# Issuing one of two row transfers from ScalarE's instruction stream instead of SyncE's, in a transformer layer on one core

## The chip, the core and the metric

The kernel runs on one core of a Trainium2 chip. A core has five engines with an instruction stream each: TensorE (PE in the rows, with its weight loads as PEld), VectorE (DVE), ScalarE (ACT), GpSimd (POOL) and SyncE (SP), which computes nothing and issues transfers. Transfers run on 16 DMA engines that all streams share. The streams meet only at semaphores. The metric is the device time of one execution in microseconds (us); lower is better.

## What is computed

A post-norm transformer layer on x of shape (4, 1024, 128) in float32: causal attention with 16 heads of size 64, a residual, a layer norm, a feed-forward part whose hidden layer of 512 passes butterfly transforms, a second residual and layer norm. The change is in the attention alone:

```python
q = einsum('BSE,EHK->BSHK', x, w_q);  k, v likewise
logits = einsum('BSHK,BMHK->BSHM', q, k) / sqrt(64)
probs = softmax(logits + causal_mask, axis=3)
out = einsum('BSHK,BMHK->BSHK', probs, v)
x = layernorm(x + einsum('BSHK,EHK->BSE', out, w_o))
```

## The kernel before

Work goes in 32 **units**: a unit is one pair of heads of one batch entry (8 units for each of 4 entries). All streams are written out by hand, unit by unit, by a function `window` on each engine; a function `flush` on each stands at the end of a batch entry (output projection, residual, statistics), so between units 8, 16 and 24 and their predecessors lies that other work.

Within a unit there are 12 steps (`STEPS`): two chunks of 512 queries, and for each the key tiles of 128 that the mask leaves. In a step TensorE makes the scores of head 0 and then of head 1, each from two matmuls: line 662 (high part of the keys by high part of the queries, into the PSUM tile `SC`) and line 666 (`KH1` by `QL`, into the same tile). ScalarE takes the exponential of each (line 867, `PR<-SC`), GpSimd masks and sums (lines 500 to 523), TensorE multiplies with the values (line 683).

**Where the maxima come in.** The softmax subtracts each query's maximum. It is known before the unit starts: while TensorE works on unit u it also computes the raw scores of unit u+1 (line 634), VectorE reduces them (lines 989 and 992) into `NEGM`, TensorE transposes that (line 639, the filler `mt`), and VectorE copies it out of PSUM into `NROW` (line 1002), 16 partitions of 128 numbers: 8 for head 0, 8 for head 1. `QL` holds, for each head, 64 partitions with the low part of the queries and one more partition, a row of 1024 numbers, for the negated maxima; against it `KH1` has a row of ones. So the matmul of line 666 adds the negated maximum to the scores at no cost, but cannot start until the row is in `QL`. **A row of `QL` lies in one partition, `NROW` in eight, so a DMA has to carry it**: two transfers of 4 KB for each unit, one a head, both from `rows` (line 394) in SyncE's stream. Both count on the semaphore `m_landed`, and TensorE waits for both before the first line 666 of a unit (line 665). Nothing else of that unit's scores can go ahead of it.

**What lies around it.** A unit is long (about 31 us); its last three steps are short. The fillers that TensorE works off between the steps are listed by step in `FILL`: at step 9 the projection `("proj", 0, 0)` (queries of a later unit) and behind it `mt`; at step 11, behind both scores, `("proj", 2, 0)`: three matmuls on lines 614 to 616, whose result ScalarE copies to `VT` (line 807). After it comes the next unit with its lines 662 and 666. ScalarE's stream has the same order: exponentials of step 10, of step 11, the copy to `VT`, then the next unit's first exponential.

**SyncE's stream** for a unit: `copies` (lines 381 and 385, four pairs of 128 KB), `inverses` of the denominators (lines 402, 406 and 409), `rows` for the next unit, and in 18 of the units `stage_weights` (line 364, 512 KB into `SW`) behind them; then the next unit's `copies`.

Of the kernel before, what the change touches and what calls it, by code (L numbers as in the profile page):

```python
# [24 lines left out]
F32 = mybir.dt.float32  # L25
# [5 lines left out]
H, K = 16, 64  # L31
PAIRS = H // 2
UNITS = B * PAIRS
TILES = S // P
# [35 lines left out]
def adds_reading(s):  # L70

    return adds_until(s + 2 if STEPS[s][1] == 0 else s + 1)
# [90 lines left out]
def post_norm_layer(nc, x, w_q, w_k, w_v, w_o, W_exp, b_exp, up_w, up_b, down_w, W_con, b_con, down_b, out):  # L163
    ctx = ExitStack()
    with ctx:
        def sb(name, shape, dt=F32):
            return ctx.enter_context(nc.sbuf_tensor(name, shape, dt))

        def sem(name):
            return ctx.enter_context(nc.semaphore(name))  # L170
# [9 lines left out]
        QL = sb("QL", [P, 2, 2, S], F32R)  # L180
# [16 lines left out]
        NROW = sb("NROW", [2 * TILES, P], F32R)  # L197
# [61 lines left out]
        negm_made, nrow_made, m_landed = sem("negm_made"), sem("nrow_made"), sem("m_landed")  # L259
# [15 lines left out]
        def lays_after(n):  # L275

            return [CHUNKS + (n - 8) // 2] if n >= 8 and n % 2 == 0 and CHUNKS + (n - 8) // 2 < len(LAY) else []
# [9 lines left out]
        def unit_at(b, j, par):  # L287
            return At(par, PAIRS, 2, b, j)
# [4 lines left out]
        FIRST, MIDDLE, PENULTIMATE, LAST = range(4)  # L293
# [10 lines left out]
        def work_base(b, j, par, kind):  # L304

            return At(len(PREFETCH) + NF * par - (kind != FIRST) - (len(EARLY) if kind == LAST else 0)
                      - (LAYS if b == B - 1 else 0), PER_BATCH, 2 * NF, b, j)
# [7 lines left out]
        def fillers(kind):  # L315

            n, made = 0, []
            for s, place, f in FILLERS:
                if kind == FIRST and f == ("norm", 1, 1):
                    continue  # L320
                if (kind == PENULTIMATE and f in EARLY) or (kind == LAST and f[0] != "norm"):
                    continue
                made.append((s, place, f, n, 1 + (f in EARLY)))
                n += 1
            return made
# [5 lines left out]
        def pair_col(j, par, ahead):  # L331

            return ((j * 2 + (par + ahead)) % PAIRS) * P
# [6 lines left out]
        def prob(unit, s, n=None):  # L340

            qc, kt = STEPS[s]
            n = CH - START[s] if n is None else n
            return PR[:, (unit.times(NS) + s) % PRING, :, 0:n]
# [5 lines left out]
        def _(sp):  # L350
# [37 lines left out]
            def rows(par, f_unit):  # L388

                sp.wait_ge(nrow_made, (f_unit + 1).value())  # L390
                for h in range(2):
                    row = K if h == 0 else 0
                    dst = QL[row:row + 1, par, h, :].rearrange("a (t c) -> a t c", t=TILES)
                    sp.dma_start(dst.bitcast(F32), NROW[h * TILES:(h + 1) * TILES, :].bitcast(F32)).then_inc(m_landed, 16)  # L394

            def inverses(unit, qc):

# [405 lines left out]
        @block.scalar  # L804
        def _(act):
            def hi(dst, src):
                return nc.scalar.activation(dst, src, ACT.Copy)  # L807

            def stage_weights(col):

                w = hi(WST[:, 0, :, :], WQKV[:, :, bass.ds(col, P)])
                w.then_inc(weights_hi, 1)

            nc.scalar.preload_act_table_set("natural_log_exp_and_others")
            def lay(n):

                act.wait_ge(laid_made, n + 1)
                hi(XTH[:, n * CH:(n + 1) * CH], lay_banks[n % 4]).then_inc(xt_hi, 1)

            for n in range(CHUNKS):
                lay(n)
            act.wait_ge(in_w, 48)
            stage_weights(0)

            def evacuate(f, at, unit, nxt):

                w, free = WORK[at.bank()], work_free[at.bank()]
                if f[0] == "proj":
                    _, n, c = f  # L830
                    act.wait_ge(work_ready, (at + 1).value())
                    cols = slice(c * CH, (c + 1) * CH)
                    A, Bh = slice(0, K), slice(K, P)
                    if n == 2:
                        hi(VT[:, c, :], w[:, :]).then_inc(free, 1)
                        return
                    T = QH if n == 0 else KHL
                    hi(T[A, nxt, 0, cols], w[A, :])
                    hi(T[Bh, nxt, 1, cols], w[Bh, :]).then_inc(qk_hi, 1)
                elif f[0] == "vt":  # L840
                    c = f[1]
                    act.wait_ge(work_ready, (at + 1).value())
                    if c == 0 and unit >= 0:

                        act.wait_ge(pv_done, (unit.times(NS) + PV_CREDIT).value())
                    hi(VP[:, nxt, c * TPC:(c + 1) * TPC, :], w[:, :].rearrange("p (t k) -> p t k", t=TPC))\
                        .then_inc(free, 1)
                elif f[0] == "norm":

                    _, qc, back = f  # L850
                    norms = (unit + -back).times(CHUNKS) + qc
                    act.wait_ge(work_ready, (at + 1).value())
                    act.wait_ge(sums_landed, (norms.times(32) + 32).value())
                    nc.scalar.activation(R0[:, :], w[:, :], ACT.Copy).then_inc(sums_out, 1)  # L854
                    act.wait_ge(sums_out, (norms + 1).value())
                    act.sem_inc(free, 1)

            def exp(unit, s, h):
                qc, kt = STEPS[s]
                n, use = CH - START[s], 2 * s + h  # L860
                act.wait_ge(scores_ready, (unit.times(2 * NS) + (use + 1)).value())
                if h == 0:

                    before, back = (s - PRING, 0) if s >= PRING else (s - PRING + NS, -NA)
                    act.wait_ge(pv_done, (unit.times(NS) + (s + 1 - PRING + PV_CREDIT)).value())
                    act.wait_ge(add_done, (unit.times(NA) + (adds_reading(before) + back + ADD_CREDIT)).value())
                nc.scalar.activation(prob(unit, s)[:, h, :], SC[use % NSC][:, 0:n], ACT.Exp,  # L867
                                     scale=K ** -0.5).then_inc(exp_done, 1)

            def window(b, j, par, kind):  # L870
                unit, base = unit_at(b, j, par), work_base(b, j, par, kind)
                queue = fillers(kind)
                for s in range(NS):
                    exp(unit, s, 0)
                    for place in range(3):
                        for f, n, ahead in [(f, n, ahead) for at, p, f, n, ahead in queue if (at, p) == (s, place)]:
                            evacuate(f, base + n, unit, (par + ahead) % 2)
                            if f == LAST_PROJ and kind in (FIRST, MIDDLE):

                                stage_weights(pair_col(j, par, 2))  # L880
                        if place == BETWEEN:
                            exp(unit, s, 1)

            act.wait_ge(rows_set, 1)
            for n, (f, ahead) in enumerate(PREFETCH):
                evacuate(f, At(n), At(-1), ahead - 1)
                for job in lays_after(n):
                    if LAY[job][0] == "x":
                        lay(job)
                if f == LAST_PROJ:  # L890
                    stage_weights(P)

            def flush(b):
                evacuate(("norm", 1, 0), flush_base(b), At(PAIRS - 1, PAIRS, 0, b), 0)
                if b >= B - 2:
                    return
                for n in range(LAYS):
                    at = flush_base(b) + (1 + NWORK + n)
                    act.wait_ge(work_ready, (at + 1).value())
                    hi(XTH[:, bass.ds(b % 2 * S + n * 2 * P, 2 * P)], WORK[at.bank()][:, 0:2 * P]).then_inc(xt_hi, 1)  # L900

            sweep(act, window, flush)

            for g in range(B * CHUNKS):
                for t_ in range(HT):
                    act.wait_ge(hid_ready, g * HT + t_ + 1)
                    if t_ == 0 and g > DOWN_LAG:
                        act.wait_ge(y_ready, g - DOWN_LAG)
                    nc.scalar.activation(G[g % (DOWN_LAG + 1)][:, t_, :], hid_banks[t_], ACT.Gelu,
                                         bias=BIAS1[:, t_:t_ + 1]).then_inc(gelu_done, 1)  # L910
# [263 lines left out]
```

## Time and profile before

| | us |
|---|---|
| median of 3 runs | 1208.28 |
| lowest, highest | 1206.38, 1210.69 |
| the profiled execution | 1209.85 |
| its span in the trace | 1207.8 |
| TensorE busy | 1124.5 (93%) |
| GpSimd, VectorE, ScalarE busy | 758.4, 728.8, 650.3 |

The rows further down are of that one profiled execution. A row of the timeline gives the start, the duration, the engine, the line and tiles, and in brackets how long the engine had been idle and for whom it waited. A row of the chain gives a piece of the way by which the end was reached: the start, the length and what it was. A suffix q (ACTq, SPq) marks an instruction that the engine's sequencer carries out itself, as a semaphore instruction or the issue of a DMA.
### The profile page before, as it was taken

What the parts mean: (1) busy time and instruction counts of PE and PEld (TensorE: products, weight loads), DVE (VectorE), ACT (ScalarE), POOL (GpSimd) and SP (SyncE); (2) the same over time, 40 slices, a digit from 0 to 9 for tenths busy, and PEclk for the clock granted to TensorE, in tenths of its full rate; (3) what the DMA queues carried; (4) which work ended last, traced back from release to release, by engine and by line L of the source; (5) the groups of instructions that cost most, each with busy time, mean ns of one, the idle gap of its engine ahead of it and who ended that gap; (6) DMA issues with size and microseconds to landing.
All of it is one profiled execution on the core that took longest, in us unless ns stands there. A gap on an engine that the chain in (4) does not pass through costs nothing.

```text
span 1207.8 us, 18944 instructions
## 1 busy us (share of the span) xinstructions
PE 1124.5 (93%) x5880; PEld 725.1 (60%) x5880; DVE 728.8 (60%) x2029; ACT 650.3 (54%) x1294; POOL 758.4 (63%) x722
## 2 busy tenths in 40 slices
PE   5899999999899999999899999999899999998897
PEld 4566555665666656565765555665765556653666
DVE  5766666665666666664566666665466666650555
ACT  3466666663466666663366666664366566643231
POOL 6377777776377767676177777777176676667102
PEclk9899999999999999999999999999999999998999
DMA  6122222221222222221222221221122222110002
GB/s 197 36 68 67 54 71 71 54 72 37 61 54 66 69 54 71 72 53 36 61 63 54 71 71 48 68 62 38 45 63 71 53 48 51 47 36 18 10 9 61
DMA packets 63633, 69.83 MB, mean 58 GB/s; under 512 B 26759, under 2 KB 35243, under 8 KB 63534
## 3 DMA queue, kind: packets, MB, share of 16 engines
q1 hardware_dynamic: 63534, 68.64, 21.9%
q8 instruction: 47, 0.77, 0.3%
q14 instruction: 52, 0.43, 0.1%
HBM read 32.15 MB, written 2.36 MB: 29 GB/s over the span
## 4 chain that ended last, share of the span: by engine, by line
PE 69%; DMA 9%; issue 6%; DVE 6%; ACT 3%; SPq 3%; POOL 3%; DVEq 0%; POOLq 0%; ACTq 0%
PE O L683 14%; PE WORK L634 12%; PE SC L666 9%; PE SC L662 9%; PE WORK L722 5%; DMA QL<-NROW 4%; PE WORK L651 4%; PE WORK L614 3%; PE WORK L616 3%; PE WORK L622 3%; PE WORK L615 3%; PE WORK L778 3%; DMA R<-RROW 2%; DMA RROW<-RCOL 2%; SPq L394 2%
## 5 line engine op out<-in xcount | busy, mean ns | idle before, releaser
L867 ACT ACTIVATE PR<-SC 128x512 f32<-128x512 f32 (+3 forms) x768 | 351.4, 490 | 273.4 <-PE SC L666 254.5
L515 POOL TENSOR_TENSOR SUM<-SUM,PR 128x1024 f32<-128x1024 f32 (+3 forms) x256 | 416.9, 1628 | 10.1
L683 PE MATMUL O<-PR,VP 128*64 128x512 f32 (+3 forms) x1536 | 293.0, 500 | 3.7 <-POOL PR L500 3.7
L666 PE MATMUL SC<-QL,KH 128*128 128x512 f32 (+3 forms) x768 | 265.1, 351 | 19.6 <-DMA QL<-NROW 19.6
L662 PE MATMUL SC<-QH,KHL 128*128 128x512 f32 (+3 forms) x768 | 268.4, 355 | 5.4 <-ACT PR L867 4.3
L500 POOL TENSOR_SCALAR_AFFINE_SELECT PR<-PR 128x256 f32<-128x256 f32 x256 | 107.0, 418 | 262.4 <-ACT PR L867 261.9
L989 DVE CUSTOM_DVE_ANT_0 WORK<-WORK,CMASK 128x128 f32<-128x128 f32 (+3 forms) x512 | 240.2, 510 | 34.2 <-PE WORK L634 34.0
L634 PE MATMUL WORK<-KHL,QH 128*128 128x512 f32 (+3 forms) x768 | 233.5, 377 | 11.5 <-DVE MP L989 6.4
L992 DVE TENSOR_REDUCE MP<-WORK 128x1 f32<-128x512 f32 x256 | 165.0, 686 | 84.1 <-PE WORK L634 84.1
L634 PEld LDWEIGHTS WORK<-KHL,QH 128*128 128x128 f32 x768 | 136.2, 190 | 97.1 <-issue 54.4
L662 PEld LDWEIGHTS SC<-QH,KHL 128*128 128x128 f32 x768 | 145.5, 189 | 81.2 <-ACT PR L867 41.2
L523 POOL TENSOR_TENSOR SUM<-PR 128x768 f32<-128x768 f32 x64 | 134.4, 2100 | 89.9 <-DVE OT L1017 89.4
L666 PEld LDWEIGHTS SC<-QL,KH 128*128 128x128 f32 x768 | 145.2, 189 | 46.3 <-DMA QL<-NROW 31.6
L683 PEld LDWEIGHTS O<-PR,VP 128*64 128x64 f32 x1536 | 90.8, 136 | 110.0 <-issue 69.4
L923 DVE TENSOR_TENSOR KHL<-WORK,KHL 64x512 fp32r<-64x512 f32 x128 | 88.1, 689 | 101.8 <-ACT KHL L807 100.8
L1017 DVE TENSOR_TENSOR OT<-O,R 128x512 f32<-128x512 f32 x64 | 44.2, 691 | 111.8 <-DMA R<-RROW 111.8
L923 DVE TENSOR_TENSOR QL<-WORK,QH 64x512 fp32r<-64x512 f32 x128 | 88.1, 688 | 17.1 <-ACT QH L807 15.2
L807 ACT ACTIVATE QH<-WORK 64x512 fp32r<-64x512 f32 x128 | 75.9, 593 | 33.8 <-PE WORK L616 32.3
L614 PE MATMUL WORK<-XTH,WST 128*128 128x512 f32 x192 | 79.1, 412 | 3.6 <-DVE WST L923 3.1
L854 ACT ACTIVATE R<-WORK 128x512 f32<-128x512 f32 x64 | 38.4, 600 | 76.4 <-PE WORK L651 76.4
L807 ACT ACTIVATE KHL<-WORK 64x512 fp32r<-64x512 f32 x128 | 75.6, 590 | 4.7 <-PE WORK L616 1.9
L616 PE MATMUL WORK<-XTL,WST 128*128 128x512 f32 x192 | 76.8, 400 | 0.0
(95 smaller groups left out, 1052.7 us busy)
## 6 DMA issues: line engine op xcount, KB each, us to landing
QH<-QH SPq DMA_DIRECT2D x128, 128.0 KB, 2.3
KH<-KHL SPq DMA_DIRECT2D x128, 128.0 KB, 2.3
R<-RROW SPq DMA_DIRECT2D x128, 128.0 KB, 2.8
SW<-in_L_ffn_up_weights_dram SPq DMA_DIRECT2D x9, 512.0 KB, 4.6
SW<-_L_ffn_down_weights_dram SPq DMA_DIRECT2D x9, 512.0 KB, 4.8
RCOL<-R SPq DMA_DIRECT2D x128, 2.0 KB, 1.8
out_dram<-X SPq DMA_DIRECT2D x8, 256.0 KB, 2.3
QL<-NROW SPq DMA_DIRECT2D x64, 4.0 KB
```

Source lines behind the costliest of these rows:

```text
L515: nc.gpsimd.tensor_tensor(total, total, prob(unit, s), ALU.add).then_inc(add_done, 1)
L523: nc.gpsimd.tensor_tensor(total, first[:, :, START[s]:], prob(unit, s), ALU.add).then_inc(add_done, 1)
L614: nc.tensor.matmul(w[:, :], WST[:, 0, n, :], XTH[:, cols], start=True, stop=False)
L634: t = nc.tensor.matmul(w[:, at_col:at_col + n], QH[:, nxt, h, qt * P:(qt + 1) * P], KHL[:, nxt, h, lo:lo + n], start=True, stop=True)
L662: nc.tensor.matmul(dst, KHL[:, par, h, kt * P:(kt + 1) * P], QH[:, par, h, q0:q0 + n], start=True, stop=False)
L666: nc.tensor.matmul(dst, KH1[:, par, h, kt * P:(kt + 1) * P], QL[:, par, h, q0:q0 + n], start=False, stop=True).then_inc(scores_ready, 1)
L683: t = nc.tensor.matmul(O[qc][h * K:(h + 1) * K, START[s]:], VP[:, par, kt, h * K:(h + 1) * K], p[:, h, :], start=kt == 0, stop=s == LAST_O ...
L807: return nc.scalar.activation(dst, src, ACT.Copy)
L867: nc.scalar.activation(prob(unit, s)[:, h, :], SC[use % NSC][:, 0:n], ACT.Exp, scale=K ** -0.5).then_inc(exp_done, 1)
L923: return nc.vector.tensor_tensor(dst, src, hi_part.bitcast(F32), ALU.subtract)
L989: op = nc.vector.tensor_tensor_reduce(cols, cols, CMASK[:, CH - n:], 1.0, LOWEST, ALU.add, ALU.max, cell)
L992: op = nc.vector.tensor_reduce(cell, cols, AX_X, ALU.max)
```

## The change

SyncE's `rows` keeps only head 0's transfer. Head 1's transfer is written as a function `row` in ScalarE's stream: it waits for the same semaphore `nrow_made`, and counts on the same `m_landed`. It stands at the end of `window`, so behind the last exponential and behind the copy to `VT`, and once ahead of all units.

```diff
@@ SyncE
             def rows(par, f_unit):
                 sp.wait_ge(nrow_made, (f_unit + 1).value())
-                for h in range(2):
-                    row = K if h == 0 else 0
-                    dst = QL[row:row + 1, par, h, :].rearrange("a (t c) -> a t c", t=TILES)
-                    sp.dma_start(dst.bitcast(F32), NROW[h * TILES:(h + 1) * TILES, :].bitcast(F32)).then_inc(m_landed, 16)
-
+                sp.dma_start(QL[K:K + 1, par, 0, :].rearrange("a (t c) -> a t c", t=TILES).bitcast(F32),
+                             NROW[0:TILES, :].bitcast(F32)).then_inc(m_landed, 16)
@@ ScalarE
+            def row(par, f_unit):
+
+                act.wait_ge(nrow_made, (f_unit + 1).value())
+                act.dma_start(QL[0:1, par, 1, :].rearrange("a (t c) -> a t c", t=TILES).bitcast(F32),
+                              NROW[TILES:2 * TILES, :].bitcast(F32)).then_inc(m_landed, 16)
+
             def window(b, j, par, kind):
...
                         if place == BETWEEN:
                             exp(unit, s, 1)
+                if kind != LAST:
+                    row(1 - par, unit + 1)
...
                 if f == LAST_PROJ:
                     stage_weights(P)
+            row(0, At(0))
```

ScalarE's stream around the end of a unit, before (L867 are exponentials, L807 copies out of PSUM; the rows from `VT` on belong to the boundary to the next unit):

```order
L867 ACTIVATE PR<-SC 128x384 x2
L807 ACTIVATE QH<-WORK 64x512 x2
L867 ACTIVATE PR<-SC 128x256 x2
L867 ACTIVATE PR<-SC 128x128 x2
L807 ACTIVATE VT<-WORK 128x512
L867 ACTIVATE PR<-SC 128x512 x2
L807 ACTIVATE KHL<-WORK 64x512 x2
```

And the same place now, where the exponentials have the line number 864, the copies 804 and the transfer 870:

```order
L864 ACTIVATE PR<-SC 128x384 x2
L804 ACTIVATE QH<-WORK 64x512 x2
L864 ACTIVATE PR<-SC 128x256 x2
L864 ACTIVATE PR<-SC 128x128 x2
L804 ACTIVATE VT<-WORK 128x512
L870 DMA QL<-NROW 1x8x128
L864 ACTIVATE PR<-SC 128x512 x2
L804 ACTIVATE KHL<-WORK 64x512 x2
```

The transfer has come between the copy to `VT` and the next unit's first exponential. SyncE's stream at the same boundary, before, from the inverses to the next unit's copies, in a unit that also fetches weights:

```order
L406 DMA RROW<-RCOL 128x8
L409 DMA R<-RROW 64x512 x2
L394 DMA QL<-NROW 1x8x128 x2
L364 DMA SW<-in_L_ffn_up_weights_dram 128x1024
L381 DMA QH<-QH 64x512 x2
```

And now:

```order
L403 DMA RROW<-RCOL 128x8
L406 DMA R<-RROW 64x512 x2
L391 DMA QL<-NROW 1x8x128
L364 DMA SW<-in_L_ffn_up_weights_dram 128x1024
L381 DMA QH<-QH 64x512 x2
```

One issue is gone from SyncE; what stands behind it is one issue nearer. The instructions of the other three engines stand in the same order as before.

## Rows read from the trace of the kernel before

**Rows 1.** The page: busy time by engine, then the costliest groups of line 666.

```profile
PE 1124.5 (93%) x5880; PEld 725.1 (60%) x5880; DVE 728.8 (60%) x2029; ACT 650.3 (54%) x1294; POOL 758.4 (63%) x722
...
L666 PE MATMUL SC<-QL,KH 128*128 128x512 f32 (+3 forms) x768 | 265.1, 351 | 19.6 <-DMA QL<-NROW 19.6
```

**Rows 2.** Waits of TensorE: waiting, waited for, us in total, times, longest us.

```profile
PE SC L666 <- DMA QL<-NROW: 19.6, 28, 1.6
```

**Rows 3.** The chain at the boundary from unit 16 to 17: start, length, what.

```profile
618.08 0.29 DVE NROW L1002
...
618.39 0.71 SPq L394
...
619.14 1.81 DMA QL<-NROW
...
620.99 0.50 PE SC L666
```

**Rows 4.** The timeline at the same boundary, from 614 us to the first scores.

```profile
614.31 2.39 POOL L515 TENSOR_TENSOR SUM<-SUM,PR 128x1024 f32<-128x1024 f32 x1
...
617.87 1.08 PE L683 MATMUL O<-PR,VP 128*64 128x512 f32 x4
...
618.39 1.45 SPq L394 DMA_DIRECT2D QL<-NROW  x2
...
619.88 0.44 SPq L364 DMA_DIRECT2D SW<-_L_ffn_down_weights_dram  x1
619.90 0.40 PE L616 MATMUL WORK<-XTL,WST 128*128 128x512 f32 x1
...
620.14 0.39 PE L662 MATMUL SC<-QH,KHL 128*128 128x512 f32 x1
620.34 0.60 ACT L807 ACTIVATE VT<-WORK 128x512 f32<-128x512 f32 x1 [0.47 <-PE WORK L616]
620.36 1.17 SPq L381 DMA_DIRECT2D QH<-QH  x2
```

**Rows 5.** Line 866 (ScalarE's semaphore instruction) between 619 and 621 us.

```profile
L866 ACTq EVENT_SEMAPHORE  x1: 38/38/38, 620.3 to 620.3; - x1
```

**Rows 6.** Line 853 (ScalarE's) and ScalarE's timeline, both around 173 us.

```profile
L853 ACTq EVENT_SEMAPHORE  x2: 17/17/17, 152.6 to 172.6; - x2
...
172.71 0.59 ACT L807 ACTIVATE VT<-WORK 128x512 f32<-128x512 f32 x1
...
174.94 0.49 ACT L867 ACTIVATE PR<-SC 128x384 f32<-128x384 f32 x1
```

**Rows 7.** Timeline at three more boundaries: 104, 956 and 1080 us.

```profile
104.78 0.60 ACT L807 ACTIVATE VT<-WORK 128x512 f32<-128x512 f32 x1 [0.47 <-PE WORK L616]
...
105.44 0.50 PE L666 MATMUL SC<-QL,KH 128*128 128x512 f32 x1 [0.47 <-DMA QL<-NROW]
...
956.01 0.60 ACT L807 ACTIVATE VT<-WORK 128x512 f32<-128x512 f32 x1 [0.47 <-PE WORK L616]
...
957.80 0.50 PE L666 MATMUL SC<-QL,KH 128*128 128x512 f32 x1 [1.60 <-DMA QL<-NROW]
...
1082.67 0.50 PE L666 MATMUL SC<-QL,KH 128*128 128x512 f32 x1 [1.59 <-DMA QL<-NROW]
```

**Rows 8.** Line 381, copies issued behind the weights (at 620), then without (at 651).

```profile
DMA to landing us min/median/max: 4.1/4.2/4.3
...
DMA to landing us min/median/max: 2.2/2.3/2.4
```

**Rows 9.** Four stretches (line 722 twice, line 666 twice): us, busy times, then PEclk, DMA share, GB/s.

```profile
296.60:304.00 7.40, 7.37 (x65) 7.18 (x64) 1.54 (x7) 0.60 (x1) 0.00 (x0) 1.00 0.11 32
844.95:853.80 8.85, 8.85 (x64) 8.66 (x64) 1.53 (x7) 0.60 (x1) 0.00 (x0) 0.82 0.21 60
957.80:961.80 4.00, 4.00 (x18) 3.35 (x19) 1.06 (x2) 3.34 (x6) 2.08 (x3) 1.00 0.19 44
1082.67:1087.00 4.33, 4.11 (x13) 2.38 (x15) 0.30 (x1) 2.07 (x4) 3.47 (x6) 0.61 0.02 4
```

## The prediction, made before the changed kernel was run

> **What bounds the kernel now.** I read the page first. TensorE is busy for 1124.5 of 1207.8 us and no other engine for more than two thirds [rows 1], so time is lost or won where TensorE stands still. One of the places where it does is the group of line 666, idle for 19.6 us behind `QL<-NROW`; by the table of waits that is 28 waits of at most 1.6 us, 0.7 us each [rows 2]. The kernel has 31 boundaries between units. At three of them `flush` lies between, and the rows are in `QL` long before they are wanted; 28 are left, and those are the 28 waits. So each ordinary boundary waits for the transfers that the change touches.
>
> The chain shows what the wait is made of [rows 3]: `NROW` is written at 618.37, SyncE issues head 0's transfer at 618.39 (0.71 us) and head 1's at 619.14, that one lands 1.81 us later, and line 666 starts 0.04 us behind it, at 620.99. Had there been no wait it would have started some 0.23 us after line 662 at 620.14 (the distance between two such matmuls, 619.90 to 620.14 [rows 4]), so 0.62 us are lost here. The timeline shows the neighbours: TensorE's last matmul of `("proj", 2, 0)` starts at 619.90, and ScalarE begins its copy to `VT` when that is done, at 620.34 [rows 4]. This order is the heart of the matter: **the copy to `VT` starts 1.2 us after SyncE issues the second transfer today**, and the change puts the transfer behind it.
>
> **The change part by part.**
>
> *One issue fewer on SyncE.* Head 0's transfer goes out as before, at 618.39, and would land at 620.20. What stands behind it on SyncE (the weights' transfer, the next copies) goes out 0.75 us earlier (619.14 less 618.39 [rows 3]). TensorE does not wait for these here, so I cost this at nothing; the cover is the work of the next unit's first steps.
>
> *Head 1's transfer on ScalarE: when is it issued?* It stands behind the copy to `VT` (order rows). Its own semaphore, `nrow_made`, has been reached at 618.37, so what counts is whether ScalarE's sequencer gets to it ahead of the copy, when the copy starts, or when it ends. The trace has no transfer on ScalarE, but it has semaphore instructions of the same sequencer. One stands exactly where the transfer is put: line 866, behind the copy to `VT`. It waits for the values matmuls of step 8 (running from 617.87, 1.08 us) and for GpSimd's sum of step 7 (from 614.31, 2.39 us) [rows 4], both done by 619.0. Yet it ran at 620.3, with the start of the copy [rows 5]. So it did not overtake an instruction that still waited. Nor does it wait for execution: line 853 stands behind an exponential that started at 174.94, and ran at 172.6, while ScalarE still had the work from 172.71 on before it [rows 6]. Both fit one rule: it goes when everything ahead has had its semaphores, done or not. For the transfer this gives 620.34.
>
> The Trainium skill (PSUM — Partial Sum Buffer, Engine vs sequencer instructions) says the same of sequencer instructions: they wait until earlier ones are dispatched, not until they are complete. By that rule, the trace agrees at 620.3 and at 172.6. The Trainium skill (Perfetto Trace Analysis, Per-engine timelines) has the sequencer free for the next instruction as soon as an activation is pushed into its wait queue; taken alone that would let a transfer overtake a waiting copy, which is the first rival.
>
> *What that costs.* From issue to the start of line 666 I take 1.81 + 0.04 = 1.85 us [rows 3], as if ScalarE issued like SyncE. At this boundary: 620.34 + 1.85 = 622.19 against 620.99, so 1.2 us more. Of the 28 waiting boundaries 27 have the copy to `VT` (the last, at 1082, has not: its window leaves that projection out). In 18 of the 27 the copy starts 0.65 to 0.67 us ahead of line 666, the first at 104.78 and the last at 1050.71 [rows 7], and each loses 1.19: 21.4 us. In the other nine the row is already late for other reasons (a late `NROW`, late inverses, a slow landing); the distances are 0.77, 1.02, 1.01, 0.98, 1.34, 1.28, 1.52, 1.60 and 1.79 (956.01 to 957.80 [rows 7]), and 9 x 1.85 less their sum of 11.3 is 5.3 us. Together **26.7 us**. At 1082 ScalarE is not late, and the second issue's 0.75 us is gained: -0.7. All of it lies on the path that sets the end: TensorE works densely before and behind, and ScalarE, VectorE and GpSimd wait for the scores.
>
> *The company of the transfer.* At 619.14 it had SyncE's queue to itself; at 620.34 the next unit's copies, and in 16 of the 27 boundaries the 512 KB of weights, are under way. What that can do is shown by the copies: 2.3 us to landing without the weights, 4.2 behind them [rows 8]. That bounds the addition at 0 to 1.9 us in the 16, and at 0 to 0.5 (2.3 less 1.81) in the 11. This is 4 KB against their 128, and the weights stand in another queue, so I take 0.4 and 0.1: 6.4 + 1.1, some **7 us** (0 to 36). SyncE is issuing at the same time; its 0.6 us per copy is within that bound.
>
> *The clock.* The wait at line 666 grows from 0.47 us of idleness to some 1.7 to 2.0. Waits of that length exist: after 1.60 us at 957.80 the granted clock stayed at 1.00, after 1.59 us at 1082.67 it averaged 0.61 over the next 4.3 us, part of it at 1.2 GHz [rows 7, 9]. A stretch hit so costs about 1.5 us: the same 64 matmuls of line 722 took 7.40 at clock 1.00 and 8.85 at 0.82 [rows 9]. With one in three of 27 hit, that is 9 x 1.4, some **12 us** (0 to 40).
>
> Sum: 26.7 - 0.7 + 7 + 12 = +45 us. On the profiled execution that is 1209.85 + 45 = 1255; it lay 1.6 us above the median of the runs, so the predicted median is 1208.28 + 45 = 1253 us.
>
> **The rivals.**
>
> *The sequencer overtakes the copy (faster).* If a transfer, unlike a semaphore instruction, is carried out as soon as its own semaphore is there, ScalarE issues at 618.4, beside SyncE, and both rows land by 620.2. Each boundary then gains what it waits today beyond 0.23 us behind line 662, up to 0.75: 19.2 us over the 28 (0.62 in the ordinary ones), so 1189 us. The point that decides is whether the issue comes before 619.14. For it: semaphores are the only sequencer work that the trace shows on ScalarE, and a transfer is another kind. Against it: line 866 at 620.3. Also, a wait written as an instruction of its own ahead of a transfer would have no force if transfers overtook such instructions. The Trainium skill (DMA: Bandwidth & Descriptors, Issuing engines are not separate DMA queues) says that a second issuing engine saves only the time to issue; that is the 0.75 of this case. Chance 0.12.
>
> *The transfer waits for the end of the copy.* Then it goes at 620.93 or later, 0.60 us behind [rows 4]: 27 x 0.6 = 16 us on top of 26.7, less company (the copies are further on, +4) and with a longer idle time for the clock (+15): +61, 1270 us. Against it is line 853. Chance 0.15.
>
> *Nothing to be measured.* The sequencer overtakes, but ScalarE takes 0.7 us longer from issue to landing than SyncE does, so the second row lands when it did. Within 0.3%. Chance 0.04.
>
> **How the numbers follow.** The case worked out above has 0.67; its own range is 1233 (company and clock at nothing) to 1283 (both about doubled). With the third case (1255 to 1285) it makes 0.82, so the range is 1231 to 1285; the faster rival is left outside. A measurement of this kernel tells about 0.3% (3.6 us) from no change. Faster by more: 0.12 and a little for a mixture, 0.13. Within: 0.05. Slower: 0.82.
>
> **What would show it.** Right: transfers from ScalarE that start with the copy to `VT`; some 1.2 us more between lines 662 and 666 at 27 boundaries; the wait of line 666 for `QL<-NROW` at 45 to 60 us in place of 19.6; the mean granted clock below the present 0.98. Wrong: transfers from ScalarE that start within 0.1 us of SyncE's, with ordinary waits under 0.2 us (first rival), or that start behind the end of the copy (second). If the issue is right and the time still differs, the terms for company and clock are mis-sized, which the time to landing and the granted clock would tell apart.

## The result, and the profile of the changed kernel

The changed kernel takes a median of 1311.6 us (1299.7 to 1319.2 over 4 runs) against 1208.3 us (1206.4 to 1210.7) for the kernel before: a ratio of 1.082, interval 1.074 to 1.090. It is slower by 103 us. The forecast of 1253 us had the sign right, but the loss is more than twice as large as the sum gave, and the time lies above the whole range. The profiled execution took 1314.4 us (span 1312.3).

The page first: busy times, the granted clock in 40 slices, the queue that has appeared for ScalarE's transfers, and the group of line 663 (line 666 of before), which answers to [rows 1].

```profile
PE 1170.8 (89%) x5880; PEld 761.4 (58%) x5880; DVE 728.6 (56%) x2029; ACT 653.6 (50%) x1294; POOL 757.1 (58%) x722
...
PEclk8799988999998999999989999988899899999899
...
q10 hardware_dynamic: 512, 0.13, 0.1%
...
L663 PE MATMUL SC<-QL,KH 128*128 128x512 f32 (+3 forms) x768 | 278.3, 368 | 79.6 <-DMA QL<-NROW 79.6
```

Two things have grown. TensorE waits 79.6 us for the row where it waited 19.6 us [rows 1, 2]. And the same 5880 matmuls keep it busy for 1170.8 us in place of 1124.5: they run slower. The mean granted clock is 0.937; before it was 0.982. The other engines do what they did. The table of waits has the same 28 waits as [rows 2], the longest now 4.5 us:

```profile
PE SC L663 <- DMA QL<-NROW: 79.6, 28, 4.5
```

The timeline at the boundary from unit 16 to 17 answers to [rows 3, 4]. Line 391 is SyncE's row transfer, line 870 ScalarE's, line 804 the copy to `VT`, and lines 659 and 663 are the former 662 and 666.

```profile
675.20 0.28 DVE L1008 CAST NROW<-WORK 16x128 fp32r<-16x128 f32 x1
675.51 0.71 SPq L391 DMA_DIRECT2D QL<-NROW  x1
...
676.26 0.43 SPq L364 DMA_DIRECT2D SW<-_L_ffn_down_weights_dram  x1
...
676.73 1.14 SPq L381 DMA_DIRECT2D QH<-QH  x2
...
677.24 0.40 PE L659 MATMUL SC<-QH,KHL 128*128 128x512 f32 x1
...
677.44 0.60 ACT L804 ACTIVATE VT<-WORK 128x512 f32<-128x512 f32 x1 [0.47 <-PE WORK L613]
677.45 0.66 ACTq L870 DMA_DIRECT2D QL<-NROW  x1
...
681.42 0.79 PE L663 MATMUL SC<-QL,KH 128*128 128x512 f32 x1 [3.78 <-DMA QL<-NROW]
```

And the next boundary, where no weights are fetched:

```profile
712.93 1.15 SPq L381 DMA_DIRECT2D QH<-QH  x2
...
713.90 0.40 PE L659 MATMUL SC<-QH,KHL 128*128 128x512 f32 x1
714.10 0.60 ACT L804 ACTIVATE VT<-WORK 128x512 f32<-128x512 f32 x1 [0.47 <-PE WORK L613]
714.11 0.63 ACTq L870 DMA_DIRECT2D QL<-NROW  x1
...
715.97 0.50 PE L663 MATMUL SC<-QL,KH 128*128 128x512 f32 x1 [1.67 <-DMA QL<-NROW]
```

In both, ScalarE's issue starts 0.01 us behind the start of the copy, and so it does at all 27 boundaries that have the copy. Without weights line 663 follows 1.86 us behind the issue (715.97 less 714.11), as forecast (1.85). With weights it follows 3.97 us behind it (681.42 less 677.45). The DMA queues between 677 and 679.5 us, from 679.5 to 681.5 us, and from 714.1 to 716.1 us (packets, MB, share of 16 engines) show where the row is meanwhile: queue 1 is SyncE's, queue 10 ScalarE's. The three fences are these windows in this order.

```profile
q1 hardware_dynamic: 165, 0.56, 83.7%
```

```profile
q1 hardware_dynamic: 140, 0.23, 48.1%
q10 hardware_dynamic: 16, 0.00, 1.7%
```

```profile
q1 hardware_dynamic: 156, 0.25, 54.6%
q10 hardware_dynamic: 16, 0.00, 1.0%
```

In the first two microseconds after the issue none of the row's 16 packets moves, while SyncE's queue keeps the engines 83.7% busy; they move only behind 679.5. Without the weights all 16 are carried inside the 2 us after the issue. Not all of that silence is delay: by the packets' own times, a row without the weights also sends its first packet only 1.29 us behind the issue and its last at 1.37. Behind the weights it is 2.25 and 3.19 (medians of the 16 boundaries 2.1 and 2.9). At 13 of these 16 all 128 packets of 4 KB that make up the weights have started before the row's last one. So the row is carried about in the order in which the transfers were issued, although it stands in another queue.

What follows each of the two waits is read from the granted clock, in windows of 5.3 us from the start of line 663 (columns as in [rows 9]):

```profile
681.40:686.70 5.30, 5.28 (x13) 4.31 (x14) 1.08 (x2) 3.40 (x6) 0.41 (x1) 0.50 0.00 0
715.95:721.25 5.30, 5.28 (x27) 3.97 (x29) 2.30 (x4) 4.60 (x9) 2.07 (x3) 1.00 0.21 48
```

Behind the long wait TensorE runs at 1.2 GHz and starts 13 matmuls where behind the short one, at 2.4 GHz, it starts 27.

**Where the 104.5 us between the two spans are.** I split each trace by the starts of lines 662 and 666 (659 and 663): the distance from a unit's first 662 to its first 666, summed over the 28 waiting boundaries, and the way from there to the next unit's first 662, summed ("inside units"). For the changed kernel that is +60.2 us at the boundaries and +36.9 inside the units, where nothing was edited; the stretches with `flush` add 6.8 (170.6 against 163.7). The same split for all kernels of the study, with two more readings: how many of the 28 boundaries are followed by half clock within 14 us (windows of the granted clock), and the time from the later row's issue to line 666, as a median, at the 16 boundaries with weights and at the others. All of it is of one profiled execution for each kernel; the ratio is of all its runs.

| kernel | ratio, interval | 28 boundaries | inside units | followed by 1.2 GHz | issue to 666, with / without weights |
|---|---|---|---|---|---|
| before | 1 | 30.7 | 842.7 | 1 | 1.85 / 1.85 |
| after | 1.082 (1.074 to 1.090) | 90.9 | 879.6 | 24 | 3.8 / 1.9 |
| e1, weights early | 1.038 (1.034 to 1.041) | 60.6 | 864.0 | 14 | 1.9 / 1.9 |
| e8, matmuls in the wait | 1.052 (1.049 to 1.056) | 91.6 | 844.1 | 0 | 3.8 / 2.1 |
| e5, both | 1.031 (1.028 to 1.034) | 63.0 | 849.2 | 1 | 1.95 / 1.9 |
| e3, behind the exponentials | 1.060 (1.056 to 1.065) | 78.7 | 870.5 | 17 | 4.2 / 2.0 |
| e12, e3 and weights early | 1.016 (1.014 to 1.019) | 44.3 | 849.9 | 4 | 2.0 / 2.0 |
| e4, late on SyncE | 1.041 (1.037 to 1.045) | 62.9 | 864.5 | 13 | 3.2 / 1.85 |
| e9, half the weights | 1.074 (1.070 to 1.078) | 81.4 | 875.4 | 22 | 3.2 / 1.9 |
| e2, before step 11 | 0.992 (0.990 to 0.995) | 20.2 | 844.6 | 1 | 2.3 / 2.3 |

### The profile page after: what moved, and what is told of

Same layout as the page of the kernel before. It is cut to its first block, busy times and chain, and to the rows that moved or that the text cites. A ratio compares the mean times of both kernels' runs of the same rounds, so it can differ in the third digit from the quotient of the medians.

```text
span 1312.3 us, 18944 instructions
## 1 busy us (share of the span) xinstructions
PE 1170.8 (89%) x5880; PEld 761.4 (58%) x5880; DVE 728.6 (56%) x2029; ACT 653.6 (50%) x1294; POOL 757.1 (58%) x722
## 3 DMA queue, kind: packets, MB, share of 16 engines
q1 hardware_dynamic: 63022, 68.50, 20.2%
## 4 chain that ended last, share of the span: by engine, by line
PE 78%; DMA 10%; issue 3%; DVE 3%; POOL 3%; ACT 2%; SPq 1%; POOLq 0%; DVEq 0%; ACTq 0%
PE O L680 19%; PE WORK L631 11%; PE SC L663 10%; PE SC L659 10%; DMA QL<-NROW 6%; PE WORK L719 5%; PE WORK L648 4%; PE WORK L611 4%; PE WORK L612 4%; PE WORK L613 4%; PE WORK L619 2%; PE WORK L775 2%; DMA R<-RROW 2%; POOL SUM L512 1%; PE SC L766 1%
## 5 line engine op out<-in xcount | busy, mean ns | idle before, releaser
L663 PE MATMUL SC<-QL,KH 128*128 128x512 f32 (+3 forms) x768 | 278.3, 368 | 79.6 <-DMA QL<-NROW 79.6
L659 PE MATMUL SC<-QH,KHL 128*128 128x512 f32 (+3 forms) x768 | 275.9, 365 | 4.7 <-ACT PR L864 4.3
L663 PEld LDWEIGHTS SC<-QL,KH 128*128 128x128 f32 x768 | 151.7, 198 | 108.5 <-DMA QL<-NROW 91.7
L659 PEld LDWEIGHTS SC<-QH,KHL 128*128 128x128 f32 x768 | 150.4, 196 | 81.2 <-ACT PR L864 41.0
L611 PE MATMUL WORK<-XTH,WST 128*128 128x512 f32 x192 | 91.5, 477 | 3.6 <-DVE WST L929 3.1
L612 PE MATMUL WORK<-XTH,WST 128*128 128x512 f32 x192 | 87.4, 455 | 0.0
L613 PE MATMUL WORK<-XTL,WST 128*128 128x512 f32 x192 | 85.7, 447 | 0.0
```

Of the source, the lines that this page charges most:

```text
L611: nc.tensor.matmul(w[:, :], WST[:, 0, n, :], XTH[:, cols], start=True, stop=False)
L612: nc.tensor.matmul(w[:, :], WST[:, 1, n, :], XTH[:, cols], start=False, stop=False)
L659: nc.tensor.matmul(dst, KHL[:, par, h, kt * P:(kt + 1) * P], QH[:, par, h, q0:q0 + n], start=True, stop=False)
L663: nc.tensor.matmul(dst, KH1[:, par, h, kt * P:(kt + 1) * P], QL[:, par, h, q0:q0 + n], start=False, stop=True).then_inc(scores_ready, 1)
```

## The experiments

Three causes were on the table: the late issue itself, the company of the weights' transfer, and TensorE's clock after a longer idle wait. The first four runs take the second and the third away, one at a time and together, and try the cure of the first.

**e1_weights_early.** The weights' transfer goes out ahead of the inverses and the row, so it has landed by the time ScalarE issues. The row is issued as late as in the changed kernel.

```diff
@@ SyncE, window, on the changed kernel
                     inverses(unit + -NORM_BACK[1], 1)
+                for n in range(2 * STAGES):
+                    ...
+                        stage_weights(n)
                 inverses(unit, 0)
                 if kind != LAST:
                     rows(1 - par, unit + 1)
-                for n in range(2 * STAGES):
-                    ...
-                        stage_weights(n)
```

> The changed kernel with one thing moved: SyncE issues the 512 KB weights transfer (SW) ahead of the inverses of the unit's first chunk instead of behind the rows, so that it has landed long before the boundary; 16 of the 27 boundaries had it under way. Theory (three terms: the late issue, the weights' company, the clock): ScalarE's issue still starts with the copy to VT, but the time from it to landing falls from 3.0 to 4.7 us in those 16 to about 1.85 us in all; the waits of line 663 fall from 79.6 to some 48 us; the low clock stays in about two thirds of the boundaries for 3.4 us each. 1208 + 27 (late issue) + 25 (clock) = 1260 us, 1245 to 1270. Rival (the time to landing grows because ScalarE's transfer is slow as such or because of the copies): the times to landing stay at 3 to 4.7 us and the time stays at 1300 to 1312 us.

Measured 1256.8 us (1253.5 to 1262.3), ratio 1.038. The boundaries fall from 90.9 to 60.6 us, and the two kinds can no longer be told apart. The boundary from unit 16 to 17, which had the 3.78 us of idleness:

```profile
654.91 0.71 SPq L391 DMA_DIRECT2D QL<-NROW  x1
...
655.67 1.16 SPq L381 DMA_DIRECT2D QH<-QH  x2
...
656.87 0.66 ACTq L870 DMA_DIRECT2D QL<-NROW  x1
...
658.75 0.50 PE L663 MATMUL SC<-QL,KH 128*128 128x512 f32 x1 [1.70 <-DMA QL<-NROW]
```

So the weights' transfer accounts for the second 2 us of the long waits; the next unit's copies are still beside the row and cost nothing that can be seen (1.9 us from issue to line 663, as without weights). Its removal gives back 55 us in all, more than the 30 us of the boundaries, because with the shorter waits fewer boundaries are followed by half clock (14 in place of 24).

**e8_busy_wait.** TensorE is kept at work while it waits: where the row is awaited, 14 (with weights) or 7 (without) matmuls are written into a score buffer that is overwritten next; their results are not used. All transfers are as in the changed kernel.

```diff
@@ TensorE, scores, on the changed kernel
+                    if s == 0 and h == 0 and unit % PAIRS:
+                        pe.wait_ge(exp_done, (unit.times(2 * NS) + 2).value())
+                        for _ in range(14 if ... else 7):
+                            nc.tensor.matmul(SC[1][:, 0:n], KHL[:, par, 0, kt * P:(kt + 1) * P],
+                                             QH[:, par, 0, q0:q0 + n], start=True, stop=True)
                     if s == 0 and h == 0:
```

> The changed kernel as it is, with the same extra matmuls in the wait: 7 at boundaries without the weights' transfer, 14 (3.2 us) at those with it. Theory: nothing changes in the transfers (3 to 4.7 us to landing behind the weights), but the half-clock stretches of the units disappear, from 126 us in all to under 30, and with them some 40 us: 1270 us, 1262 to 1280. Rival (the clock is no term of its own): 1312 us or more.

Measured 1275.3 us (1268.8 to 1275.6), ratio 1.052: with more work on TensorE the kernel is 36 us faster. Timeline at the same boundary and the window behind it (line 664 is the added work, 668 the former 663; ScalarE's issue is line 875):

```profile
654.41 0.39 PE L659 MATMUL SC<-QH,KHL 128*128 128x512 f32 x1
...
654.62 0.66 ACTq L875 DMA_DIRECT2D QL<-NROW  x1
654.63 3.36 PE L664 MATMUL SC<-QH,KHL 128*128 128x512 f32 x14
...
658.49 0.50 PE L668 MATMUL SC<-QL,KH 128*128 128x512 f32 x1 [0.49 <-DMA QL<-NROW]
```

```profile
658.45:663.75 5.30, 5.26 (x27) 3.96 (x29) 2.28 (x4) 4.59 (x9) 0.41 (x1) 1.00 0.21 49
```

The row comes as late as before (3.87 us behind its issue) and the boundaries sum to 91.6 us, no less than in the changed kernel. What has gone is the half clock, at 24 boundaries in the changed kernel and now at none, and with it the 36.9 us inside the units (1.4 left) and the 6.8 us in the stretches with `flush` (160.4 us now). That isolates the clock: what was idleness, and not the delay as such, made the matmuls behind it slow.

**e5_weights_early_busy_wait.** Both edits, with 7 added matmuls at each boundary.

> As the kernel with the weights moved ahead, and TensorE gets 7 matmuls of 512 columns more at each boundary inside a batch entry, between the first lines 662 and 666 (its numbering before), into the other score tile, which the next scores overwrite; they are work for nothing, about 1.6 us, and fit into the wait. Theory (the idle wait lowers the granted clock, and that costs more than the wait): the wait of the boundary stays in length, the clock stays at 1.00, and the kernel gets faster by the clock's term: 1208 + 27 = 1235 us, 1230 to 1245. Rival (the clock's low stretches have another cause, or cost nothing): no faster than its twin without the extra matmuls, 1260 us or above.

Measured 1247.4 us (1245.4 to 1251.1), ratio 1.031. This is nearly the late issue by itself: 37 us by the ratio, of it 32.3 at the boundaries. It lies outside what I had expected (1230 to 1245), 12 us above the figure. The rows take up to 2.4 us, and once 3.6, at some of the boundaries with weights, and 6.5 us are still lost inside the units; the rest stands unexplained.

**e2_row_before_step11.** ScalarE's row is moved up, ahead of the exponentials of step 11, where `NROW` is just ready.

```diff
@@ ScalarE, window, on the changed kernel
                 for s in range(NS):
+                    if s == NS - 1 and kind != LAST:
+                        row(1 - par, unit + 1)
                     exp(unit, s, 0)
                 ...
-                if kind != LAST:
-                    row(1 - par, unit + 1)
```

> The changed kernel with ScalarE's row transfer placed ahead of the two exponentials of step 11 instead of behind the copy to VT. Theory (a transfer on ScalarE goes out when everything ahead of it in the stream has its semaphores, and its own is there): it is issued at about the same time as SyncE's, both land 1.8 us later, and the waits of line 666 shrink from 0.62 to about 0 to 0.1 us in ordinary boundaries: 1208 - 19 = 1189 us, 1185 to 1196. Its cost is one issue of 0.65 us in ScalarE's stream ahead of the exponentials of step 11, hidden while those wait for their scores. Rival (the issue holds the exponentials up, and step 11 is on the path): each boundary gains nothing or loses 0.3 us, 1205 to 1215 us.

Measured 1200.3 us (1197.2 to 1206.7, 6 runs), ratio 0.992: faster than the kernel before, by 8 us (9 by the ratio) and not by 19; the expected range of 1185 to 1196 is missed.

```profile
613.81 0.28 DVE L1008 CAST NROW<-WORK 16x128 fp32r<-16x128 f32 x1
614.11 0.71 SPq L391 DMA_DIRECT2D QL<-NROW  x1
614.12 0.66 ACTq L870 DMA_DIRECT2D QL<-NROW  x1
...
615.86 0.39 PE L659 MATMUL SC<-QH,KHL 128*128 128x512 f32 x1
...
616.30 0.50 PE L663 MATMUL SC<-QL,KH 128*128 128x512 f32 x1
```

The two issues now stand side by side, 0.75 us are gained on the second, but the scores follow 2.19 us behind it in place of 1.85 [rows 3] (2.3 in the median of the boundaries). So 0.4 us come out of the 0.75 here, and the boundaries' sum falls by 10.5 us. The Trainium skill (DMA: Bandwidth & Descriptors, Issuing engines are not separate DMA queues) has a second issuing engine save only the time to issue. The trace gives about half of even that.

**e4_late_on_sync and e3_row_behind_exps.** These ask whether ScalarE's queue, or a late transfer on whatever queue, is what the weights delay. e4 leaves both rows on SyncE, with the weights between them. e3 puts ScalarE's row directly behind its last exponential, 1.2 us behind SyncE's row, just when e4's second row goes.

```diff
@@ e4: SyncE, window, on the kernel before
-                    rows(1 - par, unit + 1)
+                    rows(1 - par, unit + 1, (0,))
                 for n in range(2 * STAGES):
                     ...
                         stage_weights(n)
+                if kind != LAST:
+                    rows(1 - par, unit + 1, (1,))
@@ e3: ScalarE, window, on the changed kernel
                             exp(unit, s, 1)
-                if kind != LAST:
-                    row(1 - par, unit + 1)
+                            if s == NS - 1 and kind != LAST:
+                                row(1 - par, unit + 1)
```

> The kernel before, ScalarE issuing nothing; SyncE issues head 0's row, then the weights' transfer in the units that have one, then head 1's row, then the copies. So the second row goes out at most 0.45 us later than before, never behind the copy to VT, but behind 512 KB of weights on its own queue. Theory (small transfers land only when the weights in front have passed, whichever queue they are in): in the 16 boundaries with weights the time from the second issue to landing rises from 1.8 to 3.8 to 4.6 us (the copies behind the weights took 4.2), line 666 starts 2.5 to 3 us later there, the others are as before, and the clock drops at most of the 16: 1208 + 16 x 2.7 + 16 x 1.5 = 1275 us, 1260 to 1290. Rival (it is ScalarE's queue that is slow behind weights, SyncE's serves its transfers promptly): 1208 to 1220 us.

> The changed kernel with ScalarE's row transfer directly behind the last exponential of the unit, so ahead of the copy to VT. Theory (it goes when the exponential ahead of it has its semaphore): issue some 0.8 us before the copy to VT starts, at about the time at which the kernel before issues its second row, 0.3 to 0.4 us later; where weights are under way, issued ahead of it by SyncE at nrow + 0.78 us, the company may add up to 1.5 us in 16 boundaries. 1208 + 27 x 0.35 = 1217 us without company, 1217 to 1245 with it. Rival (the transfer waits for the exponential's end): 0.3 us more at each boundary, 8 us more.

Measured 1259.6 us (1252.2 to 1262.5) for e4 and 1280.9 us (1275.9 to 1287.0) for e3. The first fence is e4, the second e3, at the same boundary:

```profile
648.24 0.43 SPq L364 DMA_DIRECT2D SW<-_L_ffn_down_weights_dram  x1
...
648.71 0.70 SPq L394 DMA_DIRECT2D QL<-NROW  x1
...
652.17 0.79 PE L668 MATMUL SC<-QL,KH 128*128 128x512 f32 x1 [2.55 <-DMA QL<-NROW]
```

```profile
663.39 0.43 SPq L364 DMA_DIRECT2D SW<-_L_ffn_down_weights_dram  x1
...
663.83 0.67 ACTq L870 DMA_DIRECT2D QL<-NROW  x1
663.86 1.15 SPq L381 DMA_DIRECT2D QH<-QH  x2
...
667.90 0.50 PE L663 MATMUL SC<-QL,KH 128*128 128x512 f32 x1 [3.14 <-DMA QL<-NROW]
```

Behind the weights a row is late on either queue: 3.46 us here on SyncE's (median of the 16 boundaries 3.2), 4.07 us on ScalarE's (median 4.2). e4 came out just below its expectation (1260 to 1290) and far above its rival's 1208 to 1220. So a queue of its own does not let the row past. In the median it is even 1.0 us worse, though in e3 the copies go out beside the row and in e4 behind it; I did not separate what the copies and what the queue contribute to that. My expectation for e3 (at most 1245 us) was wrong by 36 us: I had taken the company at 1.5 us, where it is 2.2 (4.2 less 2.0), and had left the clock out.

**e12_behind_exps_weights_early** is e3 with e1's edit. The question was whether the terms add.

> ScalarE's row behind the last exponential and the weights out of the way: the late issue alone, in a smaller dose, to see whether the terms add. In the run without the weights moved, the row at boundaries without weights landed 1.95 us after its issue and line 663 started 1.26 us behind the start of the copy to VT, against 0.67 in the kernel before. Theory: the same now at all 27 boundaries, 27 x 0.6 = 16 us, and with an idle time of 1.1 us few low-clock stretches, 0 to 10 us: 1224 to 1234 us, from 1281 with the weights under way. Rival (the 1281 had another cause than the weights' company and the clock): above 1245.

Measured 1227.3 us (1224.7 to 1231.4), inside the expectation. With the row issued 0.75 us sooner than in e1 (1.2 us behind SyncE's row in place of 1.95) and no weights beside it, the idleness is about 1.1 us:

```profile
632.34 0.66 ACTq L870 DMA_DIRECT2D QL<-NROW  x1
...
634.34 0.50 PE L663 MATMUL SC<-QL,KH 128*128 128x512 f32 x1 [1.07 <-DMA QL<-NROW]
```

**e9_half_weights.** 17 of the 18 weights' transfers fetch 256 KB in place of 512 (the other half of the weights is left out).

```diff
@@ SyncE, stage_weights, on the changed kernel
+                cut = 2 * HID if n == 0 else HID
-                src = w[st:st + 1].rearrange("a k i o -> a (k i o)").broadcast_to([P, 2 * HID])
-                sp.dma_start(SW[:, :], src).then_inc(stage_in, 16)
+                src = w[st:st + 1].rearrange("a k i o -> a (k i o)")[:, 0:cut].broadcast_to([P, cut])
+                sp.dma_start(SW[:, 0:cut], src).then_inc(stage_in, 16)
```

> The changed kernel with 256 KB in place of 512 in 17 of its 18 weights transfers: the second half of each stage's butterfly weights is left out, so part of the feed-forward part works with old ones. Nothing else differs. Theory (ScalarE's row lands when the weights in front have passed, so its delay goes by their size): in the 15 boundaries concerned the time from issue to landing falls from about 3.8 us to 2.5 to 3.0, and with the shorter idle time the clock's low stretches get shorter: 1270 to 1290 us. Rival (a fixed delay of a second queue beside a broadcast from DRAM): 3.5 to 4 us as before, 1300 to 1312 us.

Measured 1295.3 us (1294.6 to 1302.1), ratio 1.074. That is outside the expectation (1270 to 1290) and below its rival's 1300. From issue to line 663 it now takes 3.2 us in the median of the boundaries with weights (3.8 in the changed kernel, 1.9 without weights). The delay shrinks with the transfer, which speaks for the row waiting until the weights' bytes are through, but not in proportion (from 1.9 to 1.3 us for half the bytes). The copies that follow are still there; whether they are the reason was not tested.

**e6_before_weights_early and e7_before_step11_weights_early** are the controls of e1's edit, on the kernel before and on e2.

> The kernel before with only the weights' transfer moved ahead of the inverses, as in the first experiment; both rows on SyncE. A control for the move itself. Theory: the rows went ahead of the weights anyway, so the move changes nothing: 1208 us, within 0.5%. If it is slower (the inverses now queue behind 512 KB), that part has to be taken off from the first experiment; if faster, the copies' 1.9 us matter.

> ScalarE's row ahead of the exponentials of step 11 and the weights moved ahead of the inverses: the two moves together. There the second row landed 2.15 us behind NROW (1.8 of a single one and 0.35 for two issues at once) where it was 2.56; the weights were no company to it, since they are issued behind. Theory: no more gain than from the row alone, 1197 to 1203 us; a further gain of 5 us or more would say that the weights hold up something else.

Measured 1207.2 us (ratio 1.001, 0.998 to 1.003) and 1201.7 us (0.995, 0.993 to 0.997). Both are as expected. Early weights bring nothing where the rows go out ahead of them anyway, so e1's 55 us are the company of the late row, and not a virtue of the edit.

**e10_nrow_first and e11_nrow_first_both_on_sync.** In step 9 VectorE copies `NROW` ahead of the subtractions into `QL`; in e10 with e2's placement, in e11 with both rows on SyncE as before.

```diff
@@ VectorE, window
-                    for _, _, f, n, ahead in [q for q in queue if q[0] == s]:
+                    mine_now = [q for q in queue if q[0] == s]
+                    if s == 9:
+                        mine_now.sort(key=lambda q: q[2] == ("proj", 0, 0))
+                    for _, _, f, n, ahead in mine_now:
```

> The kernel with ScalarE's row ahead of the exponentials of step 11 (1200 us), and VectorE copies NROW ahead of the two subtractions for the queries of step 9 (QL, 1.4 us) instead of behind them. NROW was finished 0.3 us behind the second of them; TensorE's transpose for it ran at 617.19 in the first trace, so NROW would be ready about 0.5 us earlier. Theory (NROW, issue, landing is the chain of the boundary): what is left of the waits there (20.2 us between lines 662 and 666, 6.4 of it unavoidable) shrinks by up to 0.25 us in ordinary boundaries: 1190 to 1196 us. Rival (another wait takes its place): 1198 to 1203 us.

> The kernel before with only VectorE's order changed in the same way, both rows on SyncE. The second row would be issued 0.5 us earlier and land 0.5 us earlier at 28 boundaries, where it is waited for by 0.62 us: 1208 - 14 = 1194 us, 1192 to 1200. Rival: SyncE is held up by its inverses at that time, so the rows go out when they did: 1205 to 1208 us.

Measured 1198.4 us (ratio 0.992, 0.990 to 0.994) and 1201.4 us (0.996, 0.994 to 0.998). `NROW` is ready sooner, but SyncE then still has `inverses` before `rows`: its issue follows 0.30 us behind `NROW` in place of 0.03 (medians). Both miss what I had expected (1190 to 1196, and 1192 to 1200). e10 is not to be told from e2; by e11 about half of e2's gain is to be had without ScalarE, though the two intervals overlap (0.994 to 0.998 and 0.990 to 0.995).

## Why the prediction was wrong in size and right in sign

**When ScalarE issues: right.** The whole argument from line 866 and line 853 [rows 5, 6] held to 0.01 us at 27 boundaries. The rival of an overtaking transfer and the rival of a transfer that waits for the end of the copy are both out. From issue to the scores, ScalarE's transfer alone takes what SyncE's does (1.86 against 1.85 us [rows 3]), so the "nothing to be measured" rival falls too.

**The late issue, 26.7 us: nearly right.** At the boundaries without weights line 663 is 2.07 us behind line 659; before it was 0.85 (620.99 less 620.14 [rows 3, 4]). That is +1.22 where I had 1.2. In e1, where only this is left at the boundaries, their sum is up by 29.9 us. The small term beside it, -0.7 at the last boundary, did not come: ScalarE issued there at 1184.56, 0.81 us behind SyncE's 1183.75, and line 663 followed line 659 by 2.04 us where it was 2.09 before.

**The company, 7 us: this step failed.** I had read the bound rightly: behind the weights the copies took 1.9 us longer [rows 8], which made 0 to 36 us. Then I took 0.4 us of the 1.9, since the row is 4 KB against 128 and stands in another queue. Neither reason counted. The boundaries' sum falls by 30.3 us from the changed kernel to e1, 1.9 us for each of the 16 with weights: the upper end. The nearest row was the right price and I discounted it. The Trainium skill (DMA: Bandwidth & Descriptors, Queues, rings and completion order) says that a DMA engine takes turns between its queues, but drains a whole packet of one, typically some 9 to 17 descriptors, before it switches. No run shows where such a packet begins and ends. The 512 KB of weights appear in the trace as 128 pieces of 4 KB, 8 for each of the 16 engines if they are shared out evenly (an estimate), so by that rule the row may well have to wait for all of them, and the trace is in line with that: most of the weights' pieces started before the row's first, and the row's last started 2.9 us behind its issue. Where the row is held meanwhile, in the DMA engines or ahead of them, was not separated.

**The clock, 12 us: this step failed most.** I had reckoned with one in three of the boundaries, 1.4 us each. Half clock followed 24 of the 28. The price of one held: 36.9 us inside the units by 24 is 1.5 us, and in e1 it is 21.3 by 14, 1.5 again. The share did not hold, and not even the upper end of 0 to 40 us holds the 43.7 us of units and flush together (the 6.8 us in flush are not there in e8, which has no half clock behind the waits). Part of it hangs on the company: one in three was meant for waits of 1.7 to 2.0 us, and at the boundaries with weights the wait became 2.87 to 4.53 us; in the changed kernel every one of those 16 was hit, and of the 12 others, at 1.55 to 1.98 us, eight. The rest is a share read from too few cases. Two waits of 1.6 us, one hit and one not [rows 7, 9], are what I had, and I went below the half that they showed. The kernels line up by the idleness (medians; a kernel's few longer waits are named where they matter):

| kernel | usual idleness at line 663, us | boundaries followed by 1.2 GHz |
|---|---|---|
| before | 0.47 | 1 of 28, behind a wait of 1.59 |
| e12 | 1.07 | 4 of 28, behind its four waits of 1.50 to 1.79 |
| e1 | 1.70 | 14 of 28 |
| after | 1.69, with weights 3.6 | 24 of 28 |
| e8 (delay as in after, filled with matmuls) | 0.4, at most 1.3 | 0 of 28 |

What counts is the single wait. Taken together from the twelve kernels without added matmuls, none of the 195 waits under 1.3 us was followed by half clock, 29 of the 64 from 1.3 to 1.8 us, 21 of the 26 from 1.8 to 2.8 us, and 50 of the 51 longer ones.

In e1 the waits (1.6 to 2.2 us) have about the length that I had reckoned with, and half are hit: the term should have been 20 us even without the company.

**Two slips in the working.** The upper bound of the main case, 26 us with company and clock doubled to 38, comes out at 1272 us and not at 1283, and the first rival's gain, over the 28 boundaries of the trace, at 18.8 us in place of 19.2. Neither matters for the outcome: the measured time lies above all of these.

**The sum, measured.** Late issue about 30, company about 30, clock and flush 44: 104 us, against 26 + 7 + 12. Taken by whole kernels, by their ratios, the split is alike: e5 (neither company nor clock) is 37 us above before, adding the company without the clock's loss gives e8, 26 us more, and the changed kernel stands 36 us above e8.

**The announced signs.** ScalarE's issue with the copy: seen. Some 1.2 us more between the lines: seen, at the boundaries without weights only. The wait of the line at 45 to 60 us: it is 79.6, and e1 has 49.7. A clock below 0.98: 0.937. The text named the case too: "if the issue is right and the time still differs, the terms for company and clock are mis-sized".

## What to carry to other kernels

Of a small transfer that the bound engine waits for, look at what is issued ahead of it, on whatever queue: here it was late behind 512 KB on either of the two. Price it behind a large one as the nearest transfer in the trace that stands there, without a discount for its size or its queue. Of an idle wait on TensorE, the wait is only part of the cost; here a wait of 1.7 us drew 1.5 us of slower matmuls in about half of the cases, one of 3 us in nearly all, and one under 1.3 us in none. And an instruction stream that is free on average is no free issuer: what counts is the instruction that the new issue stands behind, and here moving it up past two exponentials and a copy turned 8% lost into 0.8% gained.

## What the runs showed of the hardware that I had not expected

- A 4 KB transfer on ScalarE's queue, issued 1.2 us behind 512 KB on SyncE's queue, reached the scores 3.8 us after its issue in the median (3.97 at the boundary shown), in place of 1.9 without them; behind 256 KB it took 3.2 us. On SyncE's own queue, issued right behind the 512 KB, it took 3.2 us in the median.
- Two transfers of 4 KB issued at the same moment by SyncE and ScalarE (614.11 and 614.12) reach the scores 2.2 us later there (median 2.3), while one by itself takes 1.85.
- Adding 308 matmuls whose results nobody uses made the changed kernel 36 us faster (1.082 to 1.052), since they took the place of idleness.
- Half clock followed a single idle wait of TensorE never under 1.3 us (195 waits), in 29 of 64 cases from 1.3 to 1.8 us, and in 50 of 51 above 2.8 us.
